# The mixer's decay matrix in quarters of 64 rows, and its groups written out

## The reference

```python
g @ out_w.T, where
proj = input_states @ in_proj_w.T
gate, xBC, dt = ...                       # 8192, 8192 + 2 * 8 * 128, 128 columns
xBC = silu(causal_conv4(xBC) + conv_b)    # per channel, 4 taps
scores = einsum('bcihn,bcjhn->bcijh', C, B) * Ldec * dt
y = y_intra + y_inter + D * x
g = rmsnorm_of_group(y * silu(gate)) * norm_w
```

## Time and profile before

| | |
|---|---|
| median of 3 runs | 1913.84 us (1912.73 to 1914.36) |
| profiled execution | 1914.12 us |
| its span | 1912.4 us |
| PE matmul busy | 1818.8 us, 95% |
| DVE busy | 1339.7 us, 70% |
| ACT busy | 1164.3 us, 61% |
| POOL busy | 1436.6 us, 75% |

### The profile page before, as it was taken

How to read it: one execution, slowest core, us unless ns; L and a number is a source line. 1 busy time by engine, 2 the same in 40 slices (tenths; PEclk the granted TensorE clock), 3 DMA queues, 4 the chain that set the end, 5 groups by cost and what they waited for, 6 DMA issues and landing times.

```text
span 1912.4 us, 32260 instructions
## 1 busy us (share of the span) xinstructions
PE 1818.8 (95%) x10780; PEld 1453.8 (76%) x10780; DVE 1339.7 (70%) x1703; ACT 1164.3 (61%) x2105; POOL 1436.6 (75%) x1429
## 2 busy tenths in 40 slices
PE   6998896878999999999999999999999999999977
PEld 4776675667888888888888878888888888888866
DVE  4664555666677777786768767867777687678656
ACT  3221432368675776676677757766677577676752
POOL 4312323638997999799879978997999799979972
PEclk9997998989999999999999999999999999999999
DMA  3000001013222222232222312222222223223201
GB/s 111 1 1 24 1 1 59 12 55 112 82 92 75 78 95 99 69 98 80 89 79 78 101 67 94 99 78 80 88 79 98 69 94 100 89 72 106 77 18 45
DMA packets 107066, 136.01 MB, mean 71 GB/s; under 512 B 9026, under 2 KB 74690, under 8 KB 106884
## 3 DMA queue, kind: packets, MB, share of 16 engines
q1 hardware_dynamic: 105924, 133.63, 21.1%
q10 hardware_dynamic: 960, 0.05, 0.0%
HBM read 131.02 MB, written 2.62 MB: 70 GB/s over the span
## 4 chain that ended last, share of the span: by engine, by line
PE 75%; DVE 4%; issue 2%; POOL 1%; ACT 1%; DVEq 0%; ACTq 0%; POOLq 0%
PE ps L144 19%; PE ps L146 19%; PE ps L145 19%; PE ps L1930 6%; PE ps L1887 3%; PE ps L1931 3%; PE ps L1074 2%; DVE mix_xT L1669 1%; DVE mix_decay L1689 1%; PE ps L1915 1%; DVE mix_cb L1694 0%; PE ps L1948 0%; PE ps L116 0%; DVE mix_u L1793 0%; POOL ffn_ln_mv L72 0%
## 5 line engine op out<-in xcount | busy, mean ns | idle before, releaser
L144 PE MATMUL ps<-mix_xnT_hi,mix_w_hi 128*128 128x512 f32 x1152 | 463.0, 402 | 9.9 <-DVE mix_bT L1669 9.6
L146 PE MATMUL ps<-mix_xnT_hi,mix_w_lo 128*128 128x512 f32 x1152 | 455.1, 395 | 0.0
L145 PE MATMUL ps<-mix_xnT_lo,mix_w_hi 128*128 128x512 f32 x1152 | 454.7, 395 | 0.0
L1669 DVE SCALAR_TENSOR_TENSOR mix_xT<-ps,mix_cur,mix_xT 128x510 f32<-128x510 f32 x378 | 279.2, 745 | 143.6 <-ACT mix_xT L1484 134.7
L1395 POOL TENSOR_SCALAR_AFFINE_SELECT mix_spread<-mix_spread 128x256 f32<-128x256 f32 x512 | 313.6, 647 | 0.0
L1689 DVE TENSOR_TENSOR mix_decay<-mix_decay,mix_cb 128x1536 f32<-128x1536 f32 x128 | 291.7, 2316 | 5.5 <-ACT mix_decay L1510 4.6
L1533 ACT ACTIVATE mix_g_hi<-mix_gated 128x512 fp32r<-128x512 f32 x128 | 81.0, 633 | 324.2 <-POOL mix_gated L1372 291.1
L144 PEld LDWEIGHTS ps<-mix_xnT_hi,mix_w_hi 128*128 128x128 f32 x1152 | 217.5, 189 | 59.8 <-issue 11.8
L146 PEld LDWEIGHTS ps<-mix_xnT_hi,mix_w_lo 128*128 128x128 f32 x1152 | 217.1, 188 | 50.8
L1508 ACT ACTIVATE mix_decay<-mix_spread,mix_cur_ncum 128x256 f32<-128x256 f32 x512 | 253.8, 496 | 1.5 <-issue 1.4
L145 PEld LDWEIGHTS ps<-mix_xnT_lo,mix_w_hi 128*128 128x128 f32 x1152 | 217.7, 189 | 46.8
(11 more groups left out here) (262 smaller groups left out, 3330.0 us busy)
## 6 DMA issues: line engine op xcount, KB each, us to landing
mix_spread<-cum_rows SPq DMA_DIRECT2D x128, 512.0 KB, 4.0
mix_w_raw<-in_w_in_stream SPq DMA_DIRECT2D x144, 256.0 KB, 4.1
mix_wo_raw<-in_w_out_T SPq DMA_DIRECT2D x64, 256.0 KB, 3.5
att_w_raw<-in_w_attn_T SPq DMA_DIRECT2D x12, 256.0 KB, 3.8
x<-in_x SPq DMA_DIRECT2D x8, 256.0 KB, 4.0
out_rows<-x SPq DMA_DIRECT2D x8, 256.0 KB, 2.2
att_wp_raw<-in_w_proj_T SPq DMA_DIRECT2D x4, 256.0 KB, 2.7
mix_bT<-in_w_ffn_T SPq DMA_DIRECT2D x2, 512.0 KB, 4.9
```

Source lines behind the costliest of these rows:

```text
L144: pe.matmul(out, lh, rh, start=(k == 0), stop=False)
L145: pe.matmul(out, lh, rl, start=False, stop=False)
L146: last = pe.matmul(out, ll, rh, start=False, stop=(k == tiles - 1))
L1669: dve.scalar_tensor_tensor(out=d[:, :, shift:T], in0=src[:, :, 0:T - shift], scalar=w[:, MK - 1 - shift:MK - shift], in1=d[:, :, shift:T], ...
```

## The change

Four things:

- The columns of `decay` and `cb` are regrouped. The second 128 source tokens of a batch are put in reverse order, and each 128 x 128 source tile is cut into two quarters of 64 rows. `QUARTERS` lists for each quarter: which half of the partitions, which source tile, its first column in `decay`, and its first token t0; it is multiplied for tokens t0 to 255 only. That makes 256, 192, 128 and 64 columns. A product has 64 rows and 64 columns of the array, so that there are four tiles: two halves of the partitions times two heads.
- `y_of_pair` has two parts. In a part each half of the partitions works for one half of the batches, so for one PSUM bank, and in the other part for the other. Both banks are complete when part 1 is. Part 1 waits for the end of part 0 (`y_begun`), and between the parts stand the eight transposes, or half a product in a group's last pair.
- To have the odd tiles reversed, ACT writes a reversed copy `odd` of the odd tiles of x and of B, ahead of the silu in place; before the mixer's loop it copies the odd tiles of dt and of the sums likewise. POOL's `causal` makes two selects over 4 x 128 columns where it made four over 2 x 128.
- `over_groups` writes out all eight groups.

```diff
+HALF = P // 2
+QUARTERS = ((0, 0, 0, 0), (1, 0, HALF, HALF), (1, 1, 2 * P, P), (0, 1, 2 * P + HALF, P + HALF))
+def odd_rows(ap):
+    return ap.rearrange("p (t c) -> p t c", c=P)[:, 1::2, ::-1]
...
-        def over_groups(engine, body):
-
-            body(0, True, False)
-            with engine.Fori(1, MG - 1) as g:
-                body(g, False, False)
-            body(MG - 1, False, True)
+        def over_groups(body):
+
+            for g in range(MG):
+                body(g, g == 0, g == MG - 1)
...
-                for b in range(B):
-                    blocks = spread[:, a, b, :].rearrange("p (i c) -> p i c", c=P)
-                    last = pool.affine_select(out=blocks[:, 0::2, :], in_=blocks[:, 0:2, :], compare_op=ALU.is_ge,
-                                              fill=MASKED, base=0, pattern=[[0, 2], [1, P]], channel_multiplier=-1)
-                last.then_inc(selected, 1)
+                tile = spread[:, a, :, 0:P]
+                pool.affine_select(out=tile, in_=tile, compare_op=ALU.is_ge, fill=MASKED, base=0,
+                                   pattern=[[0, B], [1, P]], channel_multiplier=-1)
+                pool.affine_select(out=spread[:, a, :, T:BLK], in_=spread[:, a, :, P:T], compare_op=ALU.is_ge,
+                                   fill=MASKED, base=1 - P, pattern=[[0, B], [1, P]], channel_multiplier=1)\
+                    .then_inc(selected, 1)
...
-            def silu_conv(n_cv, dst):
+            def silu_conv(n_cv, dst, written=None):
+
                 act.wait_ge(convolved, 6 * (n_cv + 1))
+                if written is not None:
+                    act.activation(odd[:, :, :], odd_rows(dst), ACT.Silu).then_inc(silu_odd, 1)
+                    act.wait_ge(silu_odd, written)
                 act.activation(dst, dst, ACT.Silu).then_inc(silu_x, 1)
...
-                        dve.wait_ge(y_done, 2 * pair + half + 1)
+                        dve.wait_ge(y_done[half], pair + 1)
...
-            def y_of_pair(g, k, first):
+            def y_of_pair(g, k, first, part):
                 pair = PAIRS * g + k
-
-                at_least(pe, y_skip, 2 * pair)
-                pe.wait_ge(mixed, GHEADS * g + 2 * k + 2)
-                pe.wait_ge(aux_free, x_ready(g, k, first))
+                if part == 0:
+                    at_least(pe, y_skip, 2 * pair)
+                    pe.wait_ge(mixed, GHEADS * g + 2 * k + 2)
+                    pe.wait_ge(aux_free, x_ready(g, k, first))
+                else:
+                    pe.wait_ge(y_begun, 2 * (pair + 1))
+                last = {}
+                for j in range(2):
+                    for n, (rows, tile, col, t0) in enumerate(QUARTERS):
+                        half = part ^ rows
+                        b, r = 2 * half + j, slice(HALF * rows, HALF * rows + HALF)
+                        for a in range(2):
+                            last[half] = pe.matmul(
+                                ps[64 * a:64 * a + 64, 4 + half, j * T + t0:j * T + T],
+                                x_dt[r, 2 * b + tile, 64 * a:64 * a + 64], decay[r, a, b, col:col + T - t0],
+                                start=(part == 0 and j == 0 and n < 2), stop=(part == 1), skip_group_check=True)
                 for half in range(2):
-                    for b in (2 * half, 2 * half + 1):
-                        for a in range(2):
-                            out = ps[64 * a:64 * a + 64, 4 + half, (b % 2) * T:(b % 2 + 1) * T]
-                            m = decay[:, a, b, :]
-                            pe.matmul(out, x_dt[:, 2 * b, 64 * a:64 * a + 64], m[:, 0:T], start=True, stop=False)
-                            last = pe.matmul(out[:, P:T], x_dt[:, 2 * b + 1, 64 * a:64 * a + 64], m[:, T:BLK],
-                                             start=False, stop=True)
-                    last.then_inc(y_done, 1)
+                    last[half].then_inc(y_done[half] if part else y_begun, 1)
...
-                    y_of_pair(g, k, first)
+                    y_of_pair(g, k, first, 0)
                     if has_next and k < PAIRS - 1:
                         turn_x(n_aux(g, ("x", k, 0)), n_conv(g, ("x", k + 1)), (k + 1) % 2)
+                    elif not last:
+                        next_product(g, ("b", 0), (0,))
+                    y_of_pair(g, k, first, 1)
                 if not last:
-                    next_product(g, ("b", 0))
+                    next_product(g, ("b", 0), (1,))
```

More of the change, by code:

```diff
@@ L1197, in build_mixer @@
         DT_BANKS = (6, 7, 4, 5)
+        dt_odd, sums_odd = (xT[:, 1, n * 512:(n + 1) * 512].rearrange("p (b c) -> p b c", c=P) for n in range(2))
+        dt_reversed = sem("dt_reversed")
         block = ctx.enter_context(nc.Block())
@@ L1505, in exps @@
                     act.wait_ge(selected, GHEADS * g + hc + 1)
-                    at_least(act, y_done, 2 * (PAIRS * g + k))
+                    for half in range(2):
+                        at_least(act, y_done[half], PAIRS * g + k)
                 for b in batches:
@@ L1945, in b_dot_c @@
                     at_least(pe, aux_free, n_aux(g, ("cb", b)) - 1)
[L1946 to L1951 removed]
+                    out, t0 = aux_of(("cb", b)), b * T
+                    for n, (rows, tile, col, t) in enumerate(QUARTERS):
+                        r = slice(HALF * rows, HALF * rows + HALF)
+                        pieces = odd[:, b, r] if tile else bT[:, t0 + t:t0 + t + HALF]
+                        last = pe.matmul(out[r, col:col + T - t], pieces, cT[:, t0 + t:t0 + T],
+                                         start=(n < 2), stop=(n > 1), skip_group_check=True)
+                    last.then_inc(aux, 1)
             def body(g, first, last):
```

69 lines of the change are left out of this document (42 added, 27 removed).

## The result

The changed kernel takes **1989.11 us** (median of 4 runs, 1985.34 to 1991.57) against 1913.28 for the kernel before in the same session: a ratio of 1.0398, 95% interval 1.0381 to 1.0414. It is 76 us slower; the prediction had said 31, with a range that ended at 1982. The profiled execution has a span of 1987.6 us, 75.2 more than before.

What follows compares the result with a forecast made beforehand. PE was taken as always busy at full clock, with a chain from y through skip, gate, exponentials and mix back to y having 1.8 us to spare; terms summed to +30.7 us on 1913.84, giving 1945, range 1908 to 1982.

Steps and rivals of the forecast that it cites:

- the stream, the entry, the chain: y block: 1.13 us a part, next product at 3.50; gates and exponentials 2.00 later; PE gains 0.15 a pair.
- rival C: y block: row tiles not free of each other; 1995 us in program order, 2065 if row halves run serially; chance 0.08 together.
- the steps between groups: Pair 7 to the next group: half a product between y's parts delays the chain; +0.9 us, seven times, 6.3.
- Steady pairs: Steps 4 to 7: mixes end at 20.68, PE there at 20.41; each pair 0.18 us longer, 0.6 a group.
- rival A: DVE's mixes shrink about 1.2 us as shifted phase and fewer selects keep POOL out; 1900 us, chance 0.13 for faster.
- This step and that from 0 to 1 gain PE's 0.15 each: Steps from pair 3 to 4 and 0 to 1: no loss, PE's gain only, 14 x -0.15 = -2.1 us.
- that a wait costs what it lasts: Whole sum: delays priced by length alone, at the full granted clock, with no term for the clock.
- +0.9: Step from pair 1 to 2: DVE without rest, skip 1's 1.4 us delay counts; +0.9 us in each of 7 groups.
- +1.4: Step from pair 2 to 3: chain already sets the time, skip 1's delay counts fully; +1.4 us in 7 groups.
- Selects: POOL's two selects of 512 columns for four of 256, same elements: costed at nothing, at best a gain.
- Unrolling: Writing out the groups removes a loop cost of 0.2 us a group: -1 us, bounds 0 and -3.

Runs made afterwards that it cites:

- e2: Unrolled kernel before (old tiles, selects, no copies) with only the change's order: half of y, transposes, other half, both told of at the end; 1989.09 us, 1.0404.
- e10: Unrolled kernel before with one line changed: half 0 of y told of only with half 1, no PE instruction moved; 1942.24 us, 1.0154.
- e11: Changed kernel with both y parts back to back, transposes behind them, and four selects of 256 columns a head; 1937.89 us, 1.0140.
- e9: Changed kernel without ACT's reversed copies, so odd tiles' values are in the wrong order; 1985.34 us, 1.0387.
- e1: Kernel before with only the eight groups written out; 1915.20 us, 1.0008.
- e5: Changed kernel with DVE in pair 1 reading both sums of squares ahead of the convolution of half 0; 1963.94 us, 1.0269.
- e4: Changed kernel with useless 512-column matmuls in PE's rests, groups 1 to 7: four in pair 1, seven each in pairs 2 and 3; 1959.85 us, 1.0247.
- e13: Changed kernel with two useless 512-column matmuls ahead of the wait for the mixes, in pairs 2 and 3 alone; 1969.37 us, 1.0297.
- e8: Changed kernel with four selects of 256 columns a head in place of two of 512, same elements; 1958.46 us, 1.0226.
- e3: Changed kernel with y's part 1 straight behind part 0 and the transposes behind both; 1943.44 us, 1.0153.

## Why the prediction was right in sign and wrong in size

**Right: the stream, the entry, the chain.** Part 1.09 us, 1.25 with its exit (1.28 predicted), product at 3.52, skips, gates and exponentials (at 7.68, predicted 7.67) came out as worked out. Row tiles run together; rival C is gone. e2 shows that late telling with the old tiles is enough for a loss of this size, 12 of its 76 us being PE's own second block; e10 shows that the signal alone, half as late for half 1 (0.66 for 1.4 us), costs 30. e11 and e9 show that tiles and copies add nothing that can be told.

**Right by luck: the steps between groups**, +6.4 us for +6.3. e1 has 2.6 of them by the unrolling alone, which the prediction had taken to gain 1; only 3.8 are left for the late y.

**Steady pairs: a term mis-sized, to the good side.** The mixes were to end at 20.68; they end at 20.01 in most of these pairs, because they take 4.5 there and not 5.0, and at 20.5 in the others. That is the mechanism of rival A at work, by 0.5 of the 1.2 us that A took, and where they end at 20.01 it is enough for A's sign (before 20.35): these steps came out at -0.6 us instead of +3.8, and PE rests clearly ahead of y in two pairs of a group and not in six. Both of A's causes have a part in it: with the old selects and y told 1.3 late (e10) the mixes take 4.7, with the two long selects 4.5.

**The step that failed: "This step and that from 0 to 1 gain PE's 0.15 each".** The step 0 to 1 was put down as free of loss, with no reason given; the mixes do have 3.9 us to spare there. But another wait of PE hangs on the same late exponentials: tap, convolution, sums of squares, output row. The step measured +24.2 us in place of -1.1. e5 takes all of it away by two moved instructions. The rests of 1.33 us are 9 of the 24, and the clock is 13 by e4's steps.

**The second, and the larger by cause: that a wait costs what it lasts.** The sum has no term for the clock, though the prediction had read it as full. "+0.9" and "+1.4" for the steps 1 to 2 and 2 to 3 had two parts missing. The clock: PE's rest ahead of y lowers it, y comes 1.6 later in the next pair and the chain passes that on (2 to 3), or PE itself loses it (3 to 4). e4 prices nearly all the falls at the head of a group at 29 us, e13 those of pairs 2 and 3 at 20. And the rows added to x: the 1.4 was that of skip 1, while the mixes moved by 2.3, since the adds stretched from 5.06 to 5.94 beside GpSimd's gates and low parts. In sum, the four steps at the head of a group came out 53 us above the prediction and all other terms 9 below it. By e4's steps in place of the changed kernel's, 31 of the 53 are the clock. The other 22 are what e4 leaves: 12 in the step 0 to 1, mostly PE's rest, and 6.9 and 3.1 in the steps 1 to 2 and 2 to 3, which I put down to the adds.

**Selects: "costed at nothing".** Costed by elements, they were to be neutral or a gain. They cost, as the traces read, because an instruction of GpSimd that is twice as long holds up VectorE for longer, at a place where VectorE had nothing to spare. Most of the 30 us is the clock again, and more than half are the same us as in e13; the two are not to be added.

**Unrolling: -1 expected, +1.5 measured** (-0.4 to +3.3 by the interval), within what can be told.

**Open: when the clock falls.** The length of the rest doesn't decide it alone. Ahead of the y blocks of pairs 2 and 3 it fell in 11 of 14 places behind 1.87 to 1.91 us in the changed kernel, but in 9 of 14 in e5 and in 12 of 14 in e9 behind the same rests (1.87 to 1.92), and in none behind 1.42 to 1.59 us in e2, e8 and e13. In pair 1 it fell behind 0.50 us of rest in all seven groups of e3 and in four of e10; behind 1.33 in all seven of the changed kernel and in four of e8 (steps of 25.3 and 26.3, of 23.7 in the other three). What stood ahead of the rest differs from the y blocks: 16 matmuls of one column. No run tried what decides.

**Open: the adds.** That GpSimd's work is what stretches the adds is read from the timelines and from their 3.51 us elsewhere; no run took GpSimd's work away there.

## What to carry to other kernels

When a result comes later, follow every queue behind it to every engine, also in the steps with slack: the slack of one wait (the mixes) says nothing of another (the sums) that hangs on the same late work. If PE is busy without a gap and at the full clock, price a new gap at its length plus the matmuls that may then run at half rate; here the second was about as large as the first, and a few useless matmuls were worth 29 us. And try the signal alone before the rewrite: the one-line e10 shows that a later y costs, and in which steps, without a new tile being written (30 us for 1.3 us of lateness; the change had 2.0 and lost 76).
